# Six groups of tiles instead of five in a product-based recommendation kernel

## The reference

```python
embed = tables[arange(26)[None, :], sparse]            # [2048, 26, 32], fp32
p   = einsum('bfe,bge->bfg', embed, embed)             # 351 distinct pairs (f <= g)
l_z = einsum('bfe,feh->bh', embed, w_z)                # 26*32 -> 256
l_p = einsum('bfg,fgh->bh', p, w_p)                    # pairs -> 256
l_1 = relu(concat([l_z + l_p + l_b, dense]))
h   = relu(l_1 @ W1 + b1)                              # 269 -> 128
out = sigmoid(h @ Wf + bf)
```

## Time and profile before

| what | value |
|---|---|
| median of 3 runs | 547.92 us (547.72 to 548.17) |
| profiled execution, its own time | 549.03 us |
| its span | 547.2 us |
| VectorE busy | 419.9 us, 272 instructions |
| GpSimd busy | 407.0 us, 430 instructions |
| TensorE busy | 154.8 us, 244 matmuls |
| ScalarE busy | 81.3 us, 213 instructions |
| granted TensorE clock, mean | 0.61 |

### The profile page before, as it was taken

How to read it: one execution, slowest core, us unless ns; L and a number is a source line. 1 busy time by engine, 2 the same in 40 slices (tenths; PEclk the granted TensorE clock), 3 DMA queues, 4 the chain that set the end, 5 groups by cost and what they waited for, 6 DMA issues and landing times.

```text
span 547.2 us, 1767 instructions
## 1 busy us (share of the span) xinstructions
PE 154.8 (28%) x244; PEld 63.4 (12%) x244; DVE 419.9 (77%) x272; ACT 81.3 (15%) x213; POOL 407.0 (74%) x430
## 2 busy tenths in 40 slices
PE   0020202302234025122017005430123733155335
PEld 0000000100011001000003001110001211033213
DVE  4204099899992459999997409899999999939993
ACT  0000000000060011100024001100006310222224
POOL 6777777777777777777777777777777777777792
PEclk9996655655657557555566555865655955556556
DMA  6243434342225424323312443434232342233320
GB/s 153 16 52 25 40 32 47 38 34 32 52 13 51 50 15 52 52 20 45 52 13 22 44 50 32 38 48 52 14 51 14 43 60 34 30 40 44 43 26 14
DMA packets 44571, 21.63 MB, mean 40 GB/s; under 512 B 24448, under 2 KB 42253, under 8 KB 44557
## 3 DMA queue, kind: packets, MB, share of 16 engines
q0 software_dynamic: 13312, 6.84, 23.9%
q1 hardware_dynamic: 31246, 14.67, 10.2%
HBM read 15.14 MB, written 6.30 MB: 39 GB/s over the span
## 4 chain that ended last, share of the span: by engine, by line
POOL 67%; issue 22%; DVE 6%; DMA 2%; PE 1%; ACT 0%; SPq 0%; POOLq 0%; ACTq 0%
POOL rows L333 67%; DVE prod L399 3%; DVE pairs L413 3%; DMA rows<-in_L_rec_tables,which 1%; PE ps_h L638 1%; DMA field_rows<-passage 0%; PE ps_h L622 0%; DMA raw<-in_r_sparse_inputs 0%; DMA passage<-rows_T 0%; DVE rows_T L429 0%; PE ps_h L666 0%; SPq L289 0%; ACT scores L573 0%; PE ps_end L674 0%; ACT hidden L566 0%
## 5 line engine op out<-in xcount | busy, mean ns | idle before, releaser
L333 POOL DMA_INDIRECT rows<-in_L_rec_tables,which x416 | 394.4, 948 | 128.4 <-issue 126.0
L399 DVE TENSOR_TENSOR prod<-ps_copy,rows 128x256 f32<-128x256 f32 (+34 forms) x130 | 197.7, 1566 | 108.5 <-ACT ps_copy L514 108.3
L413 DVE TENSOR_REDUCE pairs<-prod 128x104 f32<-128x3328 f32 (+24 forms) x58 | 191.4, 3306 | 0.0
L622 PE MATMUL ps_h<-field_rows,wz 128*128 128x512 f32 (+1 forms) x120 | 81.2, 829 | 253.6 <-DMA field_rows<-passage 253.6
L514 ACT COPY ps_copy<-rows 128x256 f32<-128x256 f32 (+3 forms) x52 | 19.6, 376 | 376.1 <-DMA rows<-in_L_rec_tables,which 375.9
L622 PEld LDWEIGHTS ps_h<-field_rows,wz 128*128 128x128 f32 x120 | 32.4, 295 | 300.5 <-DMA field_rows<-passage 247.3
L638 PE MATMUL ps_h<-pair_rows,w_pair 96*128 96x512 f32 (+5 forms) x80 | 46.8, 760 | 48.1 <-ACT pair_rows L535 48.1
L535 ACT COPY pair_rows<-pairs_T 32x384 f32<-32x384 f32 (+2 forms) x84 | 31.2, 372 | 73.8 <-DVE pairs_T L441 72.9
L666 PE MATMUL ps_h<-hidden,w 128*128 128x512 f32 (+1 forms) x20 | 13.1, 788 | 65.4 <-ACT hidden L559 65.4
L638 PEld LDWEIGHTS ps_h<-pair_rows,w_pair 96*128 96x128 f32 (+2 forms) x80 | 22.5, 293 | 74.3 <-ACT pair_rows L535 39.3
L429 DVE STREAM_TRANSPOSE rows_T<-rows 128x512 f32<-128x512 f32 (+2 forms) x35 | 19.7, 562 | 0.0
(11 more groups left out here) (24 smaller groups left out, 23.3 us busy)
## 6 DMA issues: line engine op xcount, KB each, us to landing
rows<-in_L_rec_tables,which POOLq DMA_INDIRECT x416, 3.4
passage<-rows_T SPq DMA_DIRECT2D x72, 64.0 KB, 2.6
field_rows<-passage SPq DMA_DIRECT2D x18, 256.0 KB, 4.0
passage<-rows_T SPq DMA_DIRECT2D x48, 32.0 KB, 2.3
field_rows<-passage SPq DMA_DIRECT2D x12, 128.0 KB, 2.8
wz<-in_L_rec_w_z SPq DMA_DIRECT2D x1, 768.0 KB, 5.4
w_pair<-in_w_low SPq DMA_DIRECT2D x1, 288.0 KB, 5.2
w_back<-in_w_high SPq DMA_DIRECT2D x1, 288.0 KB, 5.3
```

The source lines that it names most:

```text
L333: nc.gpsimd.indirect_dma_start(rows_of(p)[:, f, k, :], None, table_rows, bass.IndirectOffsetOnAxis(ap=which[:, t, f:f + 1], axis=0),).then ...
L399: ins = nc.vector.tensor_tensor(products(p, s)[:, :, at:at + high - low, :], own.broadcast_to([P, tiles, high - low, E]), rows_of(p)[:, lo ...
L413: nc.vector.tensor_reduce(pairs[:, 0:tiles_of(p), first:end], products(p, s), AX.X, ALU.add).then_inc(summed, 1)
L622: ins = nc.tensor.matmul(across(r, ps_h0[:, h, :]), wz[:, j, h * P:(h + 1) * P], side_by_side(r, field_rows[:, j, :, :, :]), start=(j == 0 ...
```

## The change

The list of groups becomes 4, 4, 4, 2, 1, 1. The first group of one tile has plain stages, the last group ends the kernel. In the last group the fields are copied and multiplied one by one from field 8 on (units 0-3, 4-5, 6-7, then single fields). Chunk 5 (fields 20 to 23) is turned before field 23 is multiplied, and chunk 6 (fields 24, 25) right behind field 22's sums, each after a wait of VectorE for the gathered fields themselves. Field 23's sums and the third pair block (block 2) follow at once, before fields 24 and 25 are multiplied. ScalarE lays the last group's last rows before block 2 rather than behind it. GpSimd's part of the last group is 11 pairs of field 24 and 15 of field 25, on one tile.

```diff
-ABREAST = [4] * WIDE + [2, 2]
+ABREAST = [4] * WIDE + [2, 1, 1]
-ENDING = [(0, 4), (4, 8), (8, 12)] + [(f, f + 2) for f in range(12, 22, 2)] + [(f, f + 1) for f in range(22, 26)]
+ENDING = [(0, 4), (4, 6), (6, 8)] + [(f, f + 1) for f in range(8, 26)]
-STAGES = [...] * WIDE + [PLAIN, ENDING]
+STAGES = [...] * WIDE + [PLAIN, PLAIN, ENDING]
-    POOL_24 = 18
-    POOL_25 = 22
+    LAST_NS = len(STAGES[END])
+    CHUNK_5_BEFORE = 23
+    POOL_24 = 11
+    POOL_25 = 15
@@ turn_rows(r, j)
+                if r == END and j >= MOVED - 1:
+                    for u in range(unit_of(r, PER * j), unit_of(r, PER * j + n - 1) + 1):
+                        dve.wait_ge(landed[r][u], DMA * k * (UNITS[r][u][1] - UNITS[r][u][0]))
@@ VectorE's loop, last group
+            for s, (first, end) in enumerate(STAGES[END]):
+                if first == CHUNK_5_BEFORE:
+                    turn_rows(END, MOVED - 1)
+                multiply(END, s)
+                for j in range(MOVED - 1):
+                    if s == stage_of(END, PER * j + chunk_fields(j) - 1):
+                        turn_rows(END, j)
+                if s and first not in (NF - 2, NF - 1):
+                    add_and_turn(END, s - 1)
+                if first == NF - 3:
+                    turn_rows(END, CH - 1)
+                    add_and_turn(END, s)
+            for s in range(LAST_NS - 2, LAST_NS):
+                add_and_turn(END, s)
+            lay_tail(END)
@@ ScalarE, behind the units of group p
+                if p == END:
+                    lay_last_rows(p)
                 for u in range(PLACES):
                     lay_pairs(p, len(PAIR_MOVES[p]) - 2, u)
-                lay_last_rows(p)
+                if p < END:
+                    lay_last_rows(p)
```

More of the change, by code:

```diff
@@ L21 @@
 WIDE = 3
-ABREAST = [4] * WIDE + [2, 2]
+ABREAST = [4] * WIDE + [2, 1, 1]
 GROUPS = len(ABREAST)
 PLAIN = [(0, 4), (4, 8), (8, 12)] + [(f, f + 2) for f in range(12, 26, 2)]
-ENDING = [(0, 4), (4, 8), (8, 12)] + [(f, f + 2) for f in range(12, 22, 2)] + [(f, f + 1) for f in range(22, 26)]
+ENDING = [(0, 4), (4, 6), (6, 8)] + [(f, f + 1) for f in range(8, 26)]
 UNITS = [PLAIN] * (GROUPS - 1) + [ENDING]
-STAGES = [[(0, 4), (4, 8), (8, 10)] + [(f, f + 2) for f in range(10, 24, 2)] + [(24, 25), (25, 26)]] * WIDE + [PLAIN, ENDING]
+STAGES = [[(0, 4), (4, 8), (8, 10)] + [(f, f + 2) for f in range(10, 24, 2)] + [(24, 25), (25, 26)]] * WIDE + [PLAIN, PLAIN, ENDING]
 PAIRS = 351
@@ L483, in _, with add_and_turn @@
                 .then_inc(w_pair_made, 1)
-            for r in range(ROUNDS):
+            def add_and_turn(r, s):
+                add_up(r, s)
+                for m in range(len(PAIR_MOVES[r])):
+                    if stage_of(r, last_field(r, m)) == s:
+                        turn_pairs(r, m)
+            for r in range(END):
                 for s in range(len(STAGES[r]) + 1):
@@ L493, in _ @@
                     if s:
[L494 to L497, removed]
+                        add_and_turn(r, s - 1)
                 lay_tail(r)
+            for s, (first, end) in enumerate(STAGES[END]):
[13 more added lines that the diff above has]
+            lay_tail(END)
             make_hidden0_half(END)
```

## The result

The changed kernel takes 549.98 us (median of 6 runs, 549.63 to 551.03); the kernel before beside it 547.55. The ratio is 1.0047, with an interval of 1.0036 to 1.0057: 2.0 to 3.1 us slower. Its profiled execution reads 549.63 us with a span of 547.8, against 549.03 and 547.2 before. The two profiles have to be laid over each other at the start of group 3 on VectorE, 425.88 us before and 424.62 now, because the gathers of the new execution are 3 ns shorter on average (945 ns against 948), which makes 1.3 us over 416; that is chance, as the mean lies between 945 and 949 ns in the traces of this case, whichever kernel ran. From there to the end of the span it is 121.3 us before and 123.2 now. The profiled execution of the changed kernel is the fastest of its six, that of the kernel before lies above its median.

A forecast was written before the change was run, and what follows sets the result against it. GpSimd's gathers fill two thirds of the chain of waits, then VectorE's order of time counts. Without waits the span ends at 545.05 us; waits of 6.6 make 551.7, +4.5; forecast 547.92+4.5 = 552.4, range 549.3 to 555.6.

The forecast's parts named there:

- The gathers: GpSimd's row gathers: as many in the same tile order, pitch 1.25 us, ending at 524.4 us as before.
- VectorE's cost per tile: VectorE's work at 0.0336 us per pair-tile plus fixed costs: 28.4 us for the first one-tile group, 27.3 for the last.
- The change of groups: Start of the last group: VectorE waits 2.6 us (1.6 to 3.9) for ScalarE's copies, 5.45 us behind the turn.
- SyncE's queue: Chunks of the first one-tile group, back to back at 4.7 us each (4.3 to 5.3); chunk 5 landed at 512.3.
- The wait at field 9: Last group, VectorE: field 9's copy comes behind make_hidden0 of the group before; 2.9 us wait (0.6 to 6).
- the pace of the products: TensorE, first one-tile group: weight loads of 0.34 us bound matmuls on 128 columns; 20 matmuls take 7.1 us.
- rival A: Shuffle queue keeps up, chunks at 4.3 us or less: wait at field 9 is 0.6, end +2.2, 550.1; chance 0.18.
- GpSimd's share: Last group: GpSimd takes 26 pair-tiles instead of 80; 3.6 us return to VectorE, said to be on the path.
- the short tally: Closing summary of the whole kernel: without waits the end is 545.05 (-2.15), including 3.6 us back from GpSimd; waits 6.6.
- The end: Behind chunk 5's turn at 537.9: 5.6 us to the first matmul, then 8.2, so the span ends at 551.7.

The follow-up runs named there:

- e5: Changed kernel with ScalarE's copies of the last group's fields 0 to 8 made ahead of laying the previous group's pairs: 552.08 us, ratio 1.0049 to the kernel before.
- e6: As e5, with the previous group's activations moved behind the last group's copies of fields 12, 14 and 15: 549.51 us, ratio 1.0008 to the kernel before.
- e1: Kernel before with only the split into groups 4, 4, 4, 2, 1, 1, old order and GpSimd's 18 and 22 pairs: 551.16 us, ratio 1.0051.
- e7: Changed kernel with each pair product of the first one-tile group made twice: 553.91 us, ratio 1.0101 to the kernel before.
- e4: Changed kernel with 24 and 25 pairs for GpSimd instead of 11 and 15: 550.71 us, ratio 1.0048 to the kernel before.
- e11: Kernel before with GpSimd's 11 and 15 pairs and nothing else: 549.02 us, ratio 1.0029.
- e3: Changed kernel with groups 4, 4, 4, 2, 2 as before, keeping new order and GpSimd's 11 and 15 pairs: 545.06 us, ratio 0.9936 to the kernel before.
- e8: e3 with the changes of e6, copies ahead on two tiles: 546.08 us, ratio 0.9951 to the kernel before.

## Why the prediction was right, and which step failed

The direction was right, the size was 2 us too large: +4.5 forecast, +2.4 measured. The wait that I had called decisive, 2.9 of the 4.5, is not in the trace, and without it my sum is +1.6. The direction came from the rest: more work on VectorE and a second change of groups. By steps:

- **The gathers.** Right, but for the chance of 3 ns a gather.
- **VectorE's cost per tile.** Right within 2%, 1.0 us too low over the two groups: 28.4 us forecast for the first one-tile group, 28.76 in its window; 27.3 and 27.91 for the last. Some 0.6 us of it lies ahead of the turn of chunk 5 and hides that much of the wait that did not come.
- **The change of groups.** Right: 2.6 us forecast, 2.64 measured; the 12 copies took 3.35 us (3.4), the first copy came 5.5 us behind the turn (5.45). e5 and e6 show that it is a cost, but one that can be had back only with the wait behind it.
- **SyncE's queue.** Right: six chunks without a gap, 4.63 us each for my 4.7, the last landed 30.7 us behind the group's start (31.05 forecast). In e1 and e5 the same six took 5.16 and 5.17 us each. Halving the bytes saved little, as assumed: a write of 16 KB lands in 2.1 us (median), one of 32 KB in 2.3. That is 0.2 us saved where the prediction took 0.04 from the Trainium skill ("DMA: Bandwidth & Descriptors", "Anatomy of one DMA"); the fit there was made on DMAs that GpSimd issues, and these are SyncE's.
- **The wait at field 9.** Wrong here: 2.9 us forecast, none measured in the one trace there is. This is the step that failed, and in it one term, the pace of the products: I put 0.34 us on a matmul of 128 columns because each weight load is listed with 0.33. The 16 took 3.62 us, 0.22 each, at the same granted clock of 0.50, and so did their loads (16 in 3.53 us). Each of these loads is still listed with 0.333 us; but one starts 0.213 us behind the other, so they overlap, and the duration of one was never a bound on their pace. The rows of before could not show that, since products of 256 columns start 0.43 us apart, more than a load lasts. The 20 matmuls took 4.7 us where I had 7.1; the 2.4 us less and 0.4 us of a quicker queue are the 2.9, within 0.1. The rule that a matmul costs its columns, which I had cited from the Trainium skill ("TensorE: Matmul & The Clock Gate", "Step-by-step: what each phase is for") and set aside, fits: 0.22 us by halving the row of 256 columns, 0.22 measured.
- **The mechanism itself stands.** With the copies ahead (e5) the wait appears at that place, and e7 makes it with dearer products. In the changed kernel the copy of field 9 is ready about 0.1 us before VectorE wants it. With so little slack an execution whose chunks take 5.2 us each, as in e1 and e5, should have a wait of some 3 us (an estimate, six times 5.17 less 4.63). Only the fastest of the six executions was traced; that they spread over 1.4 us speaks against a full 3 us in any of them. So the time was that of rival A (550.1), but not for A's reason: the queue did not keep up, the products did. That the number agrees with A's is luck.
- **GpSimd's share.** My text and the short tally put 3.6 us of returned work on the path; the sum itself did not contain them, as it ended at chunk 5. e4 decides for the sum in the changed kernel; in the kernel before the share does count (e11).
- **The end.** Right within 0.3 as a sum: 13.8 us forecast behind the turn of chunk 5, 13.5 measured. In its parts two errors cancel, which is luck. From chunk 5's first product to the hidden layer's it is 3.5 us, where it was 5.6: 2.1 us less, not 1.5, again because the loads set no pace. Behind that it is 4.5 us where it was 5.1: 0.6 less, not 1.0, because those products ran at a granted clock of 0.98 in the profile of before (first row, window 542.20:543.60) and at 0.50 in that of the changed kernel (second row):

```profile
542.20:543.60 1.40, 1.33 (x5) 0.52 (x4) 0.48 (x1) 0.02 (x1) 0.00 (x0) 0.98 0.02 6
```
```profile
543.30:545.60 2.30, 1.78 (x6) 0.98 (x6) 0.27 (x1) 0.39 (x2) 0.00 (x0) 0.50 0.01 4
```

What the change lost lies in the split and not in the order: order and share alone are 0.9936, all of it is 1.0047, so on top of the new order the split costs 1.1%, 6.1 us. On top of the old order it costs 0.5% (e1), and in the split kernel the new order and share are worth nothing that the runs tell (1.0047 against 1.0051). The two do not add up, because both end the same wait of 7.47 us, and it can be won only once. Waits at the change of groups, taken away in e6, are 2.1 of the 6.1 us. What remains, 4.0 us, has two candidates that no run took away alone. One is VectorE's added work (56.7 us against 51.25 in e3's group, 1.75 of the difference being pairs off the path). The other is SyncE's queue, which runs without a gap through e6's last group and is 1.4 us late at chunk 5. I had priced the split and the order together and never asked for the order alone, though its gain could be read from the 7.47 us wait: it was for fields 8 to 11 landing together.

## What to carry to other kernels

When an engine waits for a batch of arrivals and has a backlog later, cut the unit that it waits for, not the group: single fields, their order and the smaller share brought 0.6%; halved groups took 1.1% away again. Every group pays a change-over on the engine that lays out its results (2.1 us here, e6), and its fixed instructions, whose part in the time was counted and not taken away by itself. Taking one wait away is worth asking for the next one in the same queue first; here the copy ahead alone brought nothing, and with the second edit 2 us. An edit that moves a copy ahead moves its wait ahead too: in e8 it held up all that stood behind it on ScalarE. A duration listed for one instruction is not its pace: loads of 0.333 us started every 0.213 us. Take the pace from starts of neighbours, in a place where nothing else holds them back, or carry both values.

## What the hardware showed beyond that

SyncE's write, wait and read of a chunk takes 3.5 us behind the last gather. While gathers run, the mean of the six chunks of the first one-tile group was between 4.6 and 5.2 us from one execution to another (six kernels with that group), single ones between 3.4 and 5.8. A kernel that hangs on this queue can differ by microseconds for it; that e5's spread of 3.6 us comes from there is likely, but one trace of it doesn't show it. Copies on ScalarE cost 0.27 us for 96 elements, 0.24 for 64 and 0.21 for 32, so a third of the size saves a fifth. The clock of TensorE at the end differs by execution, which is in none of my terms: the pair products of the last tiles ran at 0.50 in both profiles, the hidden layer's four and the last two of 128 columns took 1.22 and 0.59 us at 0.50 in the changed kernel's, and such a six took 0.75 and 0.38 us at the higher level in e6's (from 517.73).
